# 8 bit codes of x and context: VectorE multiply-add instead of ScalarE Relu in a gated cross-attention and MLP block

## The chip, the cores and the metric

The kernel runs on one core of a Trainium2 chip. The metric is the device time of one execution in microseconds (us). Engines are TensorE (PE; PEld is its weight load), VectorE (DVE), ScalarE (ACT), GpSimd (POOL) and SyncE (SP), which here only issues DMAs.

## What is computed

The reference, cut to what matters (LN is a layer norm without weights):

```python
def fake_quant(x, scale, zp):
    q = jnp.clip(jnp.round(x / scale + zp), 0.0, 255.0)
    return (q - zp) * scale
def attention(x1, x2): return fake_quant(x1, s1, z1) @ fake_quant(x2, s2, z2)

x = x + tanh(g_xattn) * attention(LN(x), ctx)     # x: 2 x 512 x 1024, ctx: 2 x 1024 x 1024
A, g = quant_act(LN(x))                           # fp8 blocks of 16, outliers twice
h = silu(A @ quant_w(w_gate).T * g) * (A @ quant_w(w_up).T * g)      # 2752 columns, int4 blocks of 16
x = x + tanh(g_ffn) * (quant_act(h) @ quant_w(w_down).T * gm)
```

Only the two fake_quant calls, on LN(x) and on ctx, are touched by the change.

## The kernel before

x is 8 tiles of 128 x 1024 (4 for each of 2 batches); ctx is 16 such tiles. Each engine has its own instruction list, written out by hand, and engines meet at semaphores; an instruction whose semaphore is late holds all that stands behind it on its engine.

Front stage (the first 83 us). SP issues the 8 loads of x (`load_x`), the parameters, then `load_ctx(0)` to `load_ctx(6)`. There are 6 context buffers, so `load_ctx(c)` from c = 6 on waits until tile c - 6 has been coded (`ctx_affine`). Behind `load_ctx(6)` SP waits at L376 for `flags_ready`: two flags, made on VectorE from the index inputs, say whether columns are permuted; SP reads both, and takes branches on them. Only then come `load_ctx(7)`, the weight pieces 0, 1 and 2 (`load_piece`, 1 in two halves of 64 partitions) mixed with `load_ctx(8)` and `load_ctx(9)`, then piece 3 and the other contexts.

A context tile goes through three engines: ScalarE turns float32 into uint8 codes (`relu_ctx`, L859, scale and bias in one Relu; the write rounds), GpSimd takes the zero point off and writes bf16 (`shift_ctx`, L702), and TensorE adds it to the column sums (`col_sums`, L1208). The byte buffer `ctx_int` has two slots, hence the wait of tile c for `ctx_quant` c - 1. An x tile goes the same way: `relu_x` on ScalarE (L867) after `layernorm(1)` or `layernorm(2)` on VectorE has made its scale and bias, `quantise_x` on VectorE (L1407, bytes to bf16), `turn_x` on TensorE (L1191), `aT_out` on ScalarE (L873). The statistics of the layer norm are `first_stats(t)` (L1367), two instructions per tile, then `aggregate`.

TensorE's list sets the order: column sums of context tiles 0 to 5, `turn_x(0)`, sums 6 and 7, `turn_x(1)`, sums 8 and 9, `attend(0)` (L1223, 16 matmuls, and L1228), sum 10, `attend(1)`, `turn_x(2)`, sums 11 to 13, `attend(2)`, and so on to `attend(7)`. `make_x1(t)` on VectorE (L1414) adds the result of `attend(t)` to x; `quantise_x(5)` stands behind `make_x1(2)` in VectorE's list, and `turn_x(5)` ahead of `attend(3)` in TensorE's. `col_lo(b)` (L1426) ends the correction term that `attend` adds last.

VectorE's list runs: statistics 0 to 2, parameters, statistics 3 to 5, flag comparisons, `aggregate` of tiles 0 to 3, flag result, `layernorm(1)`, statistics 6 and 7, `aggregate`, `quantise_x(0)`, and then the mix that the diff shows.

Behind the front: second layer norm, fp8 codes of the activations and int4 codes of the first weight pieces on ScalarE, VectorE and GpSimd (83 to 140 us), then TensorE multiplies (L1276, L1330) to the end.

Of the kernel before, what the change touches and what calls it, by code (L numbers as in the profile page):

```python
# [13 lines left out]
ALU = mybir.AluOpType  # L14
ACT = mybir.ActivationFunctionType
# [7 lines left out]
NT = ROWS // P  # L23
# [40 lines left out]
CTX_BUFS = 6  # L64


def gated_block(nc, x, ctx_in, g_xattn, g_ffn, s1, z1, s2, z2, w_gate, w_up, w_down, ri_in, ri_mid, out):
# [4 lines left out]
    with ExitStack() as ctx:  # L72
        def sb(name, shape, dt):
            return ctx.enter_context(nc.sbuf_tensor(name, shape, dt))

        def sem(name):
            return ctx.enter_context(nc.semaphore(name))
# [15 lines left out]
        x_all = big[:, 0:NT * H].rearrange("p (t h) -> p t h", t=NT)  # L93
# [5 lines left out]
        ctx_int = big[:, o:o + H // 2].bitcast(U8).rearrange("p (i n) -> p i n", i=2)  # L99
        x_int = big[:, o + H // 2:o + H].bitcast(U8).rearrange("p (i n) -> p i n", i=2)  # L100
# [23 lines left out]
        ctx_buf = [xn_all[:, 2 + b, :] for b in range(CTX_BUFS)]  # L124
# [23 lines left out]
        prm = sb("prm", [P, 8], F32)  # L148
        pinv = sb("pinv", [P, 2], F32)
# [8 lines left out]
        tt = sb("tt", [P, 8], F32)  # L158
# [5 lines left out]
        ln_mul = sb("ln_mul", [P, NT], F32)  # L164
        ln_add = sb("ln_add", [P, NT], F32)
# [31 lines left out]
        ctx_loaded = [sem(f"ctx_loaded{i}") for i in range(CTX_BUFS)]  # L197
# [6 lines left out]
        ln_ready = sem("ln_ready")  # L204
        x_affine = sem("x_affine")
        a_quant = sem("a_quant")
        a_turned = sem("a_turned")
        aT_ready = sem("aT_ready")
        ctx_affine = sem("ctx_affine")
        ctx_quant = sem("ctx_quant")  # L210
# [629 lines left out]
        def _(act):  # L840
# [7 lines left out]
            def root(n, ts):  # L848
                act.wait_ge(var_ready, n)
                act.activation(sq[:, ts], ve[:, ts], ACT.Sqrt).then_inc(sqrt_done, 1)  # L850

            def relu_ctx(c):

                w = ctx_buf[c % CTX_BUFS]
                act.wait_ge(ctx_loaded[c % CTX_BUFS], 16 * (c // CTX_BUFS) + 16)
                if c >= 2:

                    act.wait_ge(ctx_quant, c - 1)
                act.activation(ctx_int[:, c % 2, :], w, ACT.Relu, bias=prm[:, 3:4], scale=pinv[:, 1:2]).then_inc(ctx_affine, 1)  # L859

            def relu_x(t):

                act.wait_ge(ln_ready, t // 4 + 1)
                if t >= 2:

                    act.wait_ge(a_quant, t - 1)
                act.activation(x_int[:, t % 2, :], x_all[:, t, :], ACT.Relu, bias=ln_add[:, t:t + 1],  # L867
                               scale=ln_mul[:, t:t + 1]).then_inc(x_affine, 1)

            def aT_out(t):  # L870

                act.wait_ge(a_turned, t + 1)
                act.activation(aT[:, :, t * P:(t + 1) * P], tb[t % 2][:].bitcast(BF16).rearrange("p (k r) -> p k r", k=KT),  # L873
                               ACT.Copy).then_inc(aT_ready, 1)

            def col_out(b):

                act.wait_ge(colsum_done, b + 1)
                for hf in range(2):
                    last = act.activation(col_term[0:LO + 1, b, hf * MW:(hf + 1) * MW], col_bank(b, hf)[0:LO + 1, :], ACT.Copy,  # L880
                                          scale=tt[0:LO + 1, 3:4])
                last.then_inc(col_hi, 1)
# [79 lines left out]
                    act.wait_ge(h_done, n - 1)  # L962
                do_silu(n, n, PW if m[0] == "P" else UW)

            relu_ctx(0)
            relu_ctx(1)
            relu_ctx(2)
            root(1, slice(0, 4))
            relu_ctx(3)
            relu_ctx(4)  # L970
            relu_ctx(5)
            relu_x(0)
            relu_ctx(6)
            relu_ctx(7)
            relu_x(1)
            relu_ctx(8)
            relu_ctx(9)
            aT_out(0)
            relu_ctx(10)
            col_out(0)  # L980
            aT_out(1)
            relu_ctx(11)
            relu_x(2)
            relu_ctx(12)
            relu_ctx(13)
            root(2, slice(4, NT))
            relu_ctx(14)
            relu_x(3)
            relu_ctx(15)
            square_x1(0)  # L990
            aT_out(2)
            square_x1(1)
            relu_x(4)
            relu_x(5)
            relu_x(6)
            aT_out(3)
            col_out(1)
            aT_out(4)
            aT_out(5)
            square_x1(2)  # L1000
            relu_x(7)
            round_w(0, 1)
            square_x1(3)
            whole_w(0)
# [350 lines left out]
        def _(dve):  # L1355
            steps = [0]

            def step(ins):

                steps[0] += 1  # L1360
                ins.then_inc(dve_step, 1)
                dve.wait_ge(dve_step, steps[0])
# [7 lines left out]
            def aggregate(ts):  # L1370
                for t in range(ts.start, ts.stop):
                    last = dve.bn_aggr(mv[:, t, :], bst[:, t, :, :])
                step(last)
                dve.tensor_scalar(ve[:, ts], mv[:, ts, 1], EPS, None, ALU.add).then_inc(var_ready, 1)
# [6 lines left out]
            def layernorm(n, ts, mul=2.0, add=None):  # L1381


                r, m = rstd[:, ts], ln_mul[:, ts]
                dve.wait_ge(sqrt_done, n)
                step(dve.tensor_tensor(r, sq[:, ts], sq[:, ts], ALU.mult))
                step(dve.tensor_tensor(r, r, ve[:, ts], ALU.add))
                step(dve.reciprocal(r, r))
                step(dve.scalar_tensor_tensor(out=m, in0=r, scalar=mul, in1=sq[:, ts], op0=ALU.mult, op1=ALU.mult))
                if add is None:  # L1390
                    dve.tensor_tensor(ln_add[:, ts], m, n_mean[:, ts], ALU.mult).then_inc(ln_ready, 1)
                else:
                    step(dve.tensor_tensor(r, m, mv[:, ts, 0], ALU.mult))
                    dve.tensor_scalar(ln_add[:, ts], r, -1.0, add, ALU.mult, ALU.add).then_inc(ln_ready, 1)

            def first_stats(t):

                dve.wait_ge(x_loaded[t], 16)
                return stats(t)

            def quantise_x(t):

                dve.wait_ge(x_affine, t + 1)
                if t >= 2:

                    dve.wait_ge(a_turned, t - 1)
                dve.tensor_scalar(a_nat[t % 2], x_int[:, t % 2, :], nrz[:, 0:1], None, ALU.add).then_inc(a_quant, 1)  # L1407

            def make_x1(t):

                dve.wait_ge(att_done, t + 1)
                for hf in range(2):
                    xs = x_all[:, t, hf * MW:(hf + 1) * MW]
                    last = dve.scalar_tensor_tensor(out=xs, in0=acc[pair(t) + hf][:], scalar=tt[:, 0:1], in1=xs,  # L1414
                                                    op0=ALU.mult, op1=ALU.add, accum_out=x_sum[:, t, hf:hf + 1])
                last.then_inc(x1_ready, 1)
                dve.wait_ge(x1_ready, t + 1)
                dve.tensor_scalar(n_mean[:, t:t + 1], x_sum[:, t, 0:1], x_sum[:, t, 1:2], -1.0 / H, ALU.add, ALU.mult)\
                    .then_inc(mean_ready, 1)
# [168 lines left out]
            dve.tensor_scalar(tt[:, 5:6], pinv[:, 0:1], 2.0, None, ALU.mult)  # L1588
            step(dve.tensor_tensor(tt[:, 1:2], tt[:, 0:1], fz[:, 1:2], ALU.mult))
            dve.tensor_scalar(tt[:, 2:3], tt[:, 1:2], fz[:, 0:1], float(H), ALU.mult, ALU.mult).then_inc(prm_ready, 1)  # L1590
            step(first_stats(3))
            first_stats(4)
            first_stats(5)
            dve.wait_ge(idx_loaded, 32)
            dve.wait_ge(consts_made, 1)
            nm = I // 64
# [3 lines left out]
            dve.tensor_reduce(nfl[:, 0:1], neq[:, 0:8], AX_X, ALU.max).then_inc(flag_step, 1)  # L1600
            dve.tensor_reduce(nfl[0:64, 1:2], neq[0:64, 8:8 + nm], AX_X, ALU.max).then_inc(flag_step, 1)
            aggregate(slice(0, 4))
            dve.wait_ge(flag_step, 5)
            dve.tensor_reduce(nall[:, 0:1], acc[3][:, 0:2 * P], AX_X, ALU.max)
            step(dve.tensor_reduce(nall[:, 1:2], acc[3][:, P:2 * P], AX_X, ALU.max))
            dve.tensor_copy(flag[:], nall[:]).then_inc(flags_ready, 1)
            layernorm(1, slice(0, 4), tt[:, 5:6], prm[:, 1:2])
            first_stats(6)
            step(first_stats(7))
            aggregate(slice(4, NT))  # L1610
            quantise_x(0)
            dve.wait_ge(flags_ready, 1)
            in_moved = dve.value_load(flag[0:1, 0:1], min_val=0, max_val=1)
            quantise_x(1)
            col_lo(0)
            quantise_x(2)
            make_x1(0)
            layernorm(2, slice(4, NT), tt[:, 5:6], prm[:, 1:2])
            make_x1(1)
            quantise_x(3)  # L1620
            quantise_x(4)
            make_x1(2)
            quantise_x(5)
            col_lo(1)
            front_open(0)
            quantise_x(6)
            make_x1(3)
            front_open(1)
            make_x1(4)
# [251 lines left out]
```

## Time and profile before

| | |
|---|---|
| median of 3 runs | 818.23 us (816.87 to 818.39) |
| profiled execution, its own time | 818.77 us |
| its span | 817.0 us, 10350 instructions |
| PE busy | 731.0 us (89%) |
| DVE busy | 556.3 us (68%) |
| ACT busy | 311.3 us (38%), of which L859 19.5 and L867 9.7 |
| POOL busy | 343.7 us (42%), of which L702 18.4 |

Times below are from the span's start. A row of a timeline gives start, duration, engine, line, operation, output and input with their shapes, the number of instructions merged into it, and in brackets how long the engine had been idle and what ended that. A row of the chain gives start, duration, engine and line of a piece of the work that ended last, followed back.

### The profile page before, as it was taken

The numbers are of one execution on the slowest core, as the hardware profiler recorded it, in microseconds if no ns is written. First come the engines' busy times: TensorE is split into PE (matmuls) and PEld (weight loads), VectorE is DVE, ScalarE is ACT, GpSimd is POOL, SyncE is SP. The second block draws the span as 40 slices with busy tenths as digits, with TensorE's granted clock in tenths as the row PEclk, the third lists the DMA queues.
The fourth block names the chain that finished last, engine by engine and source line by source line (L and its number), as shares of the span: only waits on it lengthen the run. The fifth ranks groups of instructions, "written<-read, shape, count | busy, mean of one in ns | idle before, by whom it ended". The sixth has DMA issues, their size and how long they took to land.

```text
span 817.0 us, 10350 instructions
## 1 busy us (share of the span) xinstructions
PE 731.0 (89%) x3473; PEld 334.5 (41%) x3473; DVE 556.3 (68%) x957; ACT 311.3 (38%) x382; POOL 343.7 (42%) x206
## 2 busy tenths in 40 slices
PE   0599003999999999999999999999999999999998
PEld 0144002545444444444444444444444444444443
DVE  5459789894475756675757575745898888988800
ACT  2798972445252524343434343430222122121100
POOL 1536766769374747584848575740000000000000
PEclk9989655999999999999999999999999999999999
DMA  8910598339588897979697969774265654555320
GB/s 308 353 60 14 166 279 147 80 64 190 145 173 212 187 211 174 223 169 227 145 232 163 231 163 236 157 157 164 49 152 162 182 129 149 132 161 121 88 60 26
DMA packets 228884, 131.56 MB, mean 161 GB/s; under 512 B 201712, under 2 KB 212976, under 8 KB 227824
## 3 DMA queue, kind: packets, MB, share of 16 engines
q1 hardware_dynamic: 228848, 131.12, 65.2%
q8 instruction: 18, 0.29, 0.2%
q14 instruction: 18, 0.15, 0.1%
HBM read 61.88 MB, written 19.66 MB: 100 GB/s over the span
## 4 chain that ended last, share of the span: by engine, by line
PE 78%; DVE 5%; POOL 5%; DMA 5%; ACT 3%; SPq 2%; issue 1%; DVEq 0%
PE acc L1276 47%; PE acc L1330 27%; DMA big<-in_ctx_dram 3%; PE acc L1223 2%; POOL big L739 1%; POOL h_in L734 1%; DVE big L1535 1%; ACT wbuf_all L919 1%; POOL wbuf_all L715 1%; POOL wbuf_all L708 1%; POOL big L728 1%; DMA wbuf_all<-in_L_ffn_w_up_dram 1%; SPq L455 1%; DMA mid<-big 1%; DMA x_d<-big 1%
## 5 line engine op out<-in xcount | busy, mean ns | idle before, releaser
L1276 PE MATMUL acc<-mid 128*128 128x512 f16 x1920 | 415.1, 379 | 0.0
L1276 PEld LDWEIGHTS acc<-mid 128*128 128x128 f16 x1920 | 187.9, 98 | 226.1
L1330 PE MATMUL acc<-big,mid 128*128 128x512 f16 x1040 | 224.6, 379 | 0.0
L818 POOL TENSOR_TENSOR h_in<-wbuf_all,h_in 128x1024 f16<-128x1024 f32 (+1 forms) x56 | 114.4, 2044 | 97.2 <-ACT h_in L1115 97.1
L1330 PEld LDWEIGHTS acc<-big,mid 128*128 128x128 f16 x1040 | 101.8, 98 | 122.7
L708 POOL TENSOR_TENSOR wbuf_all<-wbuf_all,w_inv 128x1024 f32<-128x1024 f32 (+1 forms) x67 | 125.2, 1873 | 43.6 <-DVE w_inv L1448 43.6
L1558 DVE SCALAR_TENSOR_TENSOR h_out<-acc,gs,silu 128x256 f32<-128x256 f32 (+1 forms) x88 | 41.5, 471 | 102.6 <-ACT silu L956 65.3
L1442 DVE TENSOR_REDUCE tb<-wbuf_all 128x64 f32<-128x1024 f32 (+1 forms) x67 | 78.9, 1178 | 47.3 <-DMA wbuf_all<-in_L_ffn_w_gate_dram 22.2
L912 ACT ACTIVATE wbuf_all<-wbuf_all 128x1024 f32<-128x1024 f32 (+1 forms) x67 | 68.1, 1016 | 82.2 <-POOL wbuf_all L708 81.4
L1115 ACT ACTIVATE h_in<-wbuf_all 128x1024 f16<-128x1024 f32 (+1 forms) x56 | 56.9, 1016 | 103.1 <-DVE wbuf_all L1454 103.1
L1454 DVE SCALAR_TENSOR_TENSOR wbuf_all<-wbuf_all,tb 128x1024 f32<-128x1024 f32 (+1 forms) x56 | 65.1, 1163 | 0.3 <-issue 0.2
L1153 ACT ACTIVATE wbuf_all<-h_in 128x1408 f16<-128x1408 f32 x16 | 22.0, 1377 | 108.4 <-DVE h_in L1509 67.9
L956 ACT ACTIVATE silu<-acc,gs 128x256 f32<-128x256 f32 (+1 forms) x88 | 40.0, 456 | 50.2 <-PE acc L1276 49.4
L1143 ACT ACTIVATE wbuf_all<-h_in 128x1408 f32<-128x1408 f32 (+1 forms) x16 | 21.6, 1351 | 50.6 <-DVE h_in L1773 50.6
L1276 PE MATMUL acc<-big,mid 128*128 128x384 f16 x192 | 34.4, 341 | 2.1 <-DMA mid<-big 1.3
L1811 DVE SCALAR_TENSOR_TENSOR mid<-acc,hr,mid 128x512 f32<-128x512 f32 x16 | 11.4, 745 | 36.2 <-PE acc L1330 36.2
L1563 DVE TENSOR_REDUCE hm<-h_out 128x256 f32 (+2 forms) x88 | 34.0, 387 | 2.7
L1783 DVE SCALAR_TENSOR_TENSOR h_in<-wbuf_all,h_in 128x1408 f32<-128x1408 f32 (+1 forms) x16 | 25.4, 1587 | 10.1 <-ACT wbuf_all L1143 10.1
L1448 DVE RECIPROCAL w_inv<-tb 128x64 f32<-128x64 f32 (+1 forms) x56 | 30.2, 539 | 1.9
L1223 PE MATMUL acc<-mid,big 128*128 128x512 bf16 x128 | 31.5, 403 | 0.0
L702 POOL TENSOR_SCALAR mid<-big,nrz 128x1024 bf16<-128x1024 uint8 x16 | 18.4, 1151 | 30.4 <-ACT big L859 30.1
L1773 DVE SCALAR_TENSOR_TENSOR h_in<-mid,hr,h_in 128x1408 f32<-128x1408 f32 (+1 forms) x16 | 26.3, 1646 | 0.3
(159 smaller groups left out, 555.0 us busy)
## 6 DMA issues: line engine op xcount, KB each, us to landing
h_in<-h_d SPq DMA_DIRECT2D x8, 1376.0 KB, 7.0
wbuf_all<-in_L_ffn_w_gate_dram SPq DMA_DIRECT2D x21, 512.0 KB, 4.3
wbuf_all<-in_L_ffn_w_up_dram SPq DMA_DIRECT2D x21, 512.0 KB, 4.3
h_d<-h_out SPq DMA_DIRECT2D x80, 128.0 KB, 3.5
big<-in_ctx_dram SPq DMA_DIRECT2D x16, 512.0 KB, 10.7
wbuf_all<-in_L_ffn_w_down_dram SPq DMA_DIRECT2D x16, 512.0 KB, 4.5
big<-in_x_dram SPq DMA_DIRECT2D x8, 512.0 KB, 6.9
x_d<-big SPq DMA_DIRECT2D x8, 512.0 KB, 4.8
```

Source lines behind the costliest of these rows:

```text
L708: pool.tensor_tensor(w, w, spread(w_inv[0:rows, b, 0:cols // BLK]), ALU.mult).then_inc(w_scaled, 1)
L818: last = pool.tensor_tensor(nat[s % 4][:, H:H + cols], wbuf[:, s % 4, 0:cols], nat[s % 4][:, 0:cols], ALU.subtract)
L912: act.activation(wbuf[0:rows, b, 0:cols], wbuf[0:rows, b, 0:cols], ACT.Copy, bias=MAGIC, scale=W_UP)\
L956: act.activation(silu[:, m % 2, 0:cols], acc[m % 4][:, 0:cols], ACT.Silu, scale=gs[:, 2:3]).then_inc(silu_done, 1)
L1115: act.activation(nat[s % 4][:, 0:cols], wbuf[:, s % 4, 0:cols], ACT.Copy).then_inc(nat_hi, 1)
L1223: pe.matmul(acc[pair(t) + hf][:], aT[:, k, t * P:(t + 1) * P], ctxq[:, b * KT + k, hf * MW:(hf + 1) * MW], start=(k == 0), stop=False)
L1276: last = pe.matmul(acc[m % 4][:, 0:cols], left[:, k, s * P:(s + 1) * P], w[:, right, k, 0:cols], start=(k == 0 and left is a_hi and right ...
L1330: last = pe.matmul(acc[2 * i + hf][:], left[:, k - ks.start, :], right[:, k, hf * MW:(hf + 1) * MW], start=(k == 0 and left is hi and righ ...
L1442: dve.tensor_reduce(top, blocks(wbuf[0:rows, b, 0:cols]), AX_X, ALU.max, apply_absolute_value=True).then_inc(scale_step, 1)
L1454: dve.scalar_tensor_tensor(out=w, in0=w, scalar=MAGIC, in1=spread(block_scale(b, looped)[0:rows, 0:cols // BLK]), op0=ALU.subtract, op1=AL ...
L1558: dve.scalar_tensor_tensor(out=h_out[:, m % 2, 0:cols], in0=acc[m % 4][:, cols:2 * cols], scalar=gs[:, 2:3], in1=silu[:, m % 2, 0:cols], o ...
L1563: dve.tensor_reduce(hm[:, s, bass.ds(at, cols // BLK)], blocks(h_out[:, m % 2, 0:cols]), AX_X, ALU.max, apply_absolute_value=True).then_in ...
```

## The change

The 16 `relu_ctx` and 8 `relu_x` leave ScalarE's list. VectorE gets 16 `code_ctx` and 8 `code_x`: a `tensor_scalar` of 128 x 1024, float32 to uint8, multiply by one per-partition scalar and add another. Semaphores are the same; `code_x` needs no wait for `a_quant`, which is VectorE's own. In VectorE's list `first_stats(4)` to `(7)` move behind the flag result and `layernorm(1)`, `code_ctx(0)` to `code_ctx(3)` stand ahead of them, and `quantise_x(0)` to `(4)` and `layernorm(2)` move a little against `make_x1`. Nothing changes on SP, GpSimd and TensorE.

```diff
-            def relu_ctx(c):
-                w = ctx_buf[c % CTX_BUFS]
-                act.wait_ge(ctx_loaded[c % CTX_BUFS], 16 * (c // CTX_BUFS) + 16)
-                if c >= 2:
-                    act.wait_ge(ctx_quant, c - 1)
-                act.activation(ctx_int[:, c % 2, :], w, ACT.Relu, bias=prm[:, 3:4], scale=pinv[:, 1:2]).then_inc(ctx_affine, 1)
...
-            relu_ctx(0)
-            relu_ctx(1)
-            relu_ctx(2)
             root(1, slice(0, 4))
-            relu_ctx(3)
...
+            def code_ctx(c):
+                dve.wait_ge(ctx_loaded[c % CTX_BUFS], 16 * (c // CTX_BUFS) + 16)
+                if c >= 2:
+                    dve.wait_ge(ctx_quant, c - 1)
+                dve.tensor_scalar(ctx_int[:, c % 2, :], ctx_buf[c % CTX_BUFS], pinv[:, 1:2], prm[:, 3:4], ALU.mult, ALU.add)\
+                    .then_inc(ctx_affine, 1)
+
+            def code_x(t):
+                if t % 4 == 0:
+                    dve.wait_ge(ln_ready, t // 4 + 1)
+                dve.tensor_scalar(x_int[:, t % 2, :], x_all[:, t, :], ln_mul[:, t:t + 1], ln_add[:, t:t + 1], ALU.mult, ALU.add)\
+                    .then_inc(x_affine, 1)
...
+            code_ctx(0)
             step(first_stats(3))
-            first_stats(4)
-            first_stats(5)
+            code_ctx(1)
             dve.wait_ge(idx_loaded, 32)
...
             aggregate(slice(0, 4))
+            code_ctx(2)
             dve.wait_ge(flag_step, 5)
             dve.tensor_reduce(nall[:, 0:1], acc[3][:, 0:2 * P], AX_X, ALU.max)
             step(dve.tensor_reduce(nall[:, 1:2], acc[3][:, P:2 * P], AX_X, ALU.max))
             dve.tensor_copy(flag[:], nall[:]).then_inc(flags_ready, 1)
+            code_ctx(3)
             layernorm(1, slice(0, 4), tt[:, 5:6], prm[:, 1:2])
+            code_ctx(4)
+            code_x(0)
+            first_stats(4)
+            code_ctx(5)
+            quantise_x(0)
+            first_stats(5)
+            code_ctx(6)
             first_stats(6)
+            code_ctx(7)
+            code_x(1)
             step(first_stats(7))
+            code_ctx(8)
+            quantise_x(1)
             aggregate(slice(4, NT))
-            quantise_x(0)
+            code_ctx(9)
             dve.wait_ge(flags_ready, 1)
             in_moved = dve.value_load(flag[0:1, 0:1], min_val=0, max_val=1)
-            quantise_x(1)
+            code_x(2)
+            code_ctx(10)
+            quantise_x(2)
             col_lo(0)
-            quantise_x(2)
+            code_ctx(11)
+            code_x(3)
+            layernorm(2, slice(4, NT), tt[:, 5:6], prm[:, 1:2])
+            code_ctx(12)
+            quantise_x(3)
             make_x1(0)
-            layernorm(2, slice(4, NT), tt[:, 5:6], prm[:, 1:2])
+            code_ctx(13)
+            code_x(4)
+            code_ctx(14)
+            quantise_x(4)
+            code_ctx(15)
             make_x1(1)
-            quantise_x(3)
-            quantise_x(4)
+            code_x(5)
+            code_x(6)
             make_x1(2)
             quantise_x(5)
             col_lo(1)
             front_open(0)
             quantise_x(6)
+            code_x(7)
             make_x1(3)
```

## Rows read from the trace of the kernel before

**Rows 1.** Page, part 2: busy tenths in 40 slices of 20.4 us.
```profile
PE   0599003999999999999999999999999999999998
DMA  8910598339588897979697969774265654555320
```

**Rows 2.** Busy time by stretch: stretch, length, us (instructions) per engine, clock, DMA.
```profile
18.70:40.20 21.50, 11.60 (x37) 3.59 (x38) 8.81 (x17) 16.31 (x15) 11.69 (x10) 0.96 1.02 356
40.20:60.20 20.00, 19.43 (x100) 8.29 (x98) 10.72 (x27) 19.31 (x24) 6.71 (x6) 0.88 0.19 75
60.20:83.00 22.80, 22.80 (x170) 10.34 (x168) 21.79 (x45) 19.87 (x26) 14.24 (x7) 1.00 0.07 24
83.00:109.60 26.60, 0.02 (x1) 0.00 (x0) 19.55 (x33) 24.91 (x27) 16.47 (x10) 0.56 0.69 197
```

**Rows 3.** Chain of work that ended last, 12 to 64 us: start, us, what.
```profile
12.58 12.54 DMA big<-in_ctx_dram
26.17 10.50 DMA big<-in_ctx_dram
36.70 1.25 ACT big L859
38.03 1.13 POOL mid L702
...
40.24 5.97 PE acc L1223 x16
...
53.12 3.45 PE acc L1223 x16
...
57.14 1.44 DVE big L1414 x4
...
60.16 3.45 PE acc L1223 x16
```

**Rows 4.** Timeline of SP's DMA issues: context tiles 6 and 7, weight piece 4.
```profile
20.01 0.34 SPq L354 DMA_DIRECT2D big<-in_ctx_dram  x1
...
22.50 0.35 SPq L354 DMA_DIRECT2D big<-in_ctx_dram  x1
...
79.58 0.33 SPq L412 DMA_DIRECT2D wbuf_all<-in_L_ffn_w_gate_dram  x1
```

**Rows 5.** DMA view of the same three issues, in that order: KB, us to landing.
```profile
big<-in_ctx_dram SPq DMA_DIRECT2D x1, 512.0 KB, 6.3
...
big<-in_ctx_dram SPq DMA_DIRECT2D x1, 512.0 KB, 5.0
...
wbuf_all<-in_L_ffn_w_gate_dram SPq DMA_DIRECT2D x1, 512.0 KB, 3.2
```

**Rows 6.** Timeline of DVE.
```profile
12.32 3.81 DVE L1367 BATCH_NORM_STATS2 bst<-big 128x6 f32<-128x512 f32 x6
...
17.43 0.42 DVE L1604 TENSOR_REDUCE nall<-acc 128x1 f32<-128x256 f32 x1 [0.31 <-PE acc L1183]
...
18.09 0.17 DVE L1606 CAST flag<-nall 128x2 int32<-128x2 f32 x1
...
22.86 0.90 DVE L1387 TENSOR_TENSOR rstd<-rstd,ve 128x4 f32<-128x4 f32 x1
...
29.86 0.74 DVE L1407 TENSOR_SCALAR silu<-big,nrz 128x1024 bf16<-128x1024 uint8 x1
...
41.69 1.41 DVE L1426 SCALAR_TENSOR_TENSOR big<-acc,tt,big 1x512 f16<-1x512 f32 x2 [9.56 <-ACT big L880]
...
48.56 0.16 DVE L1387 TENSOR_TENSOR rstd<-rstd,ve 128x4 f32<-128x4 f32 x1
...
111.27 0.49 DVE L1549 TENSOR_SCALAR h_in<-h_in,gs 128x512 f32<-128x512 f32 x1
```

**Rows 7.** Timeline of POOL: two shifts of context tiles.
```profile
22.62 2.35 POOL L702 TENSOR_SCALAR mid<-big,nrz 128x1024 bf16<-128x1024 uint8 x2 [0.23 <-ACT big L859]
```

**Rows 8.** Timeline of ACT: the first three context tiles.
```profile
18.74 3.79 ACT L859 ACTIVATE big<-big,prm,pinv 128x1024 uint8<-128x1024 f32 x3 [6.16 <-DMA big<-in_ctx_dram]
```

More of the change, by code:

```diff
@@ L850, in root @@
                 act.activation(sq[:, ts], ve[:, ts], ACT.Sqrt).then_inc(sqrt_done, 1)
-            def relu_ctx(c):
-                w = ctx_buf[c % CTX_BUFS]
-                act.wait_ge(ctx_loaded[c % CTX_BUFS], 16 * (c // CTX_BUFS) + 16)
-                if c >= 2:
-                    act.wait_ge(ctx_quant, c - 1)
-                act.activation(ctx_int[:, c % 2, :], w, ACT.Relu, bias=prm[:, 3:4], scale=pinv[:, 1:2]).then_inc(ctx_affine, 1)
[L861 to L868, printed above, removed]
             def aT_out(t):
@@ L963, in silu_open @@
                 do_silu(n, n, PW if m[0] == "P" else UW)
-            relu_ctx(0)
-            relu_ctx(1)
-            relu_ctx(2)
             root(1, slice(0, 4))
-            relu_ctx(3)
[L970 to L977, printed above, removed]
             aT_out(0)
-            relu_ctx(10)
             col_out(0)
             aT_out(1)
[L982 to L985, printed above, removed]
             root(2, slice(4, NT))
-            relu_ctx(14)
-            relu_x(3)
-            relu_ctx(15)
             square_x1(0)
@@ L992, in _ @@
             square_x1(1)
-            relu_x(4)
-            relu_x(5)
-            relu_x(6)
             aT_out(3)
@@ L1000, in _ @@
             square_x1(2)
-            relu_x(7)
             round_w(0, 1)
```

## The prediction

> **What bounds the kernel now.** I read the page's slices first. TensorE is full from 140 us to the end, and nothing of the change lies there [rows 1]; the change acts in the first 83 us, so what counts is whether the end of the front stage moves, since what follows hangs on it through data and not through a clock time. Then the busy times by stretch [rows 2]. From 18.7 to 40.2 us the DMA engines are busy all the time (share 1.02) and no engine is full. From 40.2 to 60.2 TensorE is busy 19.4 of 20 us, though ScalarE is too (19.3); from 60.2 to 83.0 TensorE is busy 22.8 of 22.8 us. From 83.0 to 109.6 ScalarE has 24.9 of 26.6 us, with work that the change leaves as it is. Two full engines side by side are told apart by the chain [rows 3]: up to 36.7 us it is loads of context (10.5 us for tile 9), then one code pass of 1.25 us, one shift, and from 40.24 us TensorE's attend steps. ScalarE is full in the middle, but it is not what the others wait for. So its 24 Relus (29.2 us) are worth at most the one of 1.25 us that stands in the chain.
>
> **What a code pass costs on VectorE.** No row shows float32 to uint8 there. The nearest are bytes to bf16, 1024 columns, 0.74 us, and float32 to float32, 512 columns, 0.49 us [rows 6]. The first carries the same number of columns, and the second shows that float32 input runs at a similar rate: with about 0.15 us of it fixed (a 4-column step has 0.16), 1024 columns are 0.15 + 2 x 0.34 = 0.83 us. I take 0.75; bounds are 0.74 and, if bytes out halve the rate, 0.15 + 4 x 0.28 = 1.3 us. 24 passes are 18 us (to 31) on an engine that in 18.7 to 60.2 us had 19.5 of 41.5 us busy. It fits on average; the order decides.
> [...] No row here has float32 to bytes.
>
> **What the order costs: the flags.** Before, VectorE did statistics 3 to 5 from 12.32 us (0.64 each instruction) while it waited for nothing, the flag result ran at 17.43, and the flag cast ended at 18.26 us [rows 6]. Now `code_ctx(0)` stands ahead of statistics 3 and waits for the first context tile, which lands at 18.7 us [rows 8]. Then: code 0 to 19.5; statistics 3 to 20.75; code 1 to 21.5; comparisons and reduces, small steps of 0.15 to 0.2, and aggregate, to 22.4 or, held by a shift (below), 23.0 to 23.7; code 2 to 23.7 or 24.45; flag reduces 0.6, cast 0.17. `flags_ready` comes at 25.1 to 25.9 in place of 18.26, at best 24.3 if nothing is held.
> SP has issued context tile 6 and stands at that wait, with tile 7, the weight pieces, and every later load queued behind it. Before, the flags had long been there, and reading them and branching took from 20.35 to 22.50 us, that is 2.15 us [rows 4]. Now tile 7 is issued at 25.1 to 25.9 + 2.15 = 27.3 to 28.0 us. Tile 6, issued at 19.6, lands at 26.3 as before, so the DMA queue is empty by then; a load into an empty queue takes 3.2 us [rows 5]. Tile 7 lands at 30.5 to 31.2 in place of 27.5: +3.0 to +3.7. Tile 9 landed 36.67 - 27.5 = 9.2 us behind tile 7, with DMA busy throughout [rows 2, 3]; kept, it lands at 39.7 to 40.4.
>
> **GpSimd and VectorE hold each other.** L1387 took 0.90 us at 22.86 and 0.16 at 48.56; the first ended at 23.76, when the first of the two shifts begun at 22.62 (1.15 us each or so) ended [rows 6, 7]. The same op alone is short, so a VectorE op of such a kind waits out a shift, up to 1.1 us. Every code pass starts a shift on GpSimd, so what comes two places behind it can be held; one directly behind starts first, since an instruction follows on its own engine without a gap, and a shift 0.1 us after its semaphore.
> [...]
>
> **The sum on VectorE.** With cast at 25.1: code 3 to 25.8; layernorm(1), one step held, to 28.0; code 4, code_x(0) to 29.45; statistics 4 to 30.7; code 5, quantise(0) to 32.15; statistics 5 to 33.4; code 6 to 34.15; statistics 6 to 35.35; code 7, code_x(1) to 36.85; statistics 7 to 38.1; code 8, quantise(1) to 39.55; aggregate, its last step held, to 40.9; code 9 to 41.6 (tile 9 is there by 40). With the cast at 25.9 it is 42.4. Shift 9 (1.13), two column sums and attend(0) follow: 44.0 to 44.7 us in place of 40.24 [rows 3], +3.7 to +4.5. Loads and VectorE end within 2 us of each other there, so either alone would cost 2.5 us and more.
> Then TensorE: attend(0) 6.0 + 0.5 at the low clock as before, sum 10, attend(1), turn, sums, attend(2) to 61.0 to 61.8 us, where it was 57.12. Beside it VectorE does code_x(2) (held once), codes 10 to 15, col_lo(0) 1.4, layernorm(2) (held), code_x(3) to (6), quantise(2) to (4) and make_x1(0), (1) at about 1.6 each: back to back from 41.6 it reaches make_x1(2) at 61 to 62.5. So it is late by 0 to 1 us against attend(2); I take 0.6. make_x1(2), quantise(5), turn and attend(3) take 3.04 us (57.12 to 60.16) as before. code_x(7) 0.75 falls where VectorE waited 0.84 us for ScalarE in `col_lo(1)`, which now need not: nothing. attend(3) to (7) run back to back on TensorE, and what follows moves with them.
> What is gained: 1.25 to 0.75 us in the chain once, already in the sum. ScalarE's freed 29 us lie beside other work. Total +3.7 to +4.5, mean 4.1, and 0.6: +4.7 us. On the profiled execution that is 818.8 + 4.7 = 823.5; it was 0.5 above the median, so 822.9 against 818.23.
>
> **Rivals.**
> [...] 0.13.
> (b) The pass runs at half the rate, 1.3 us. 23 passes up to quantise(5) add 12 us, less some holding: +13, 831 us. Against it stands bytes in at 0.74. 0.05.
> (c) No change: the slow stretch from tile 7 to 9 (2.5 MiB in 9.2 us) runs at the rate of the loads ahead of it (1.3 us for 0.5 MiB, 6.4 us), which wins 2.8 us back, and VectorE is not held. About 819, 0.12.
> [...] 0.08.
> That the codes are not what the Relu gave (rounding, negatives) would change values and no time.
>
> **How the numbers follow.** Forecast 822.9, with its own range 820.5 to 825, chance 0.62. The range to hold the time 8 times in 10 goes to most of (a) and to the lower edge of the forecast and part of (c): 819.5 to 828; left out are (d), (b) and half of (c). A measurement of this kernel tells 0.2% (1.6 us) from nothing. Slower: forecast, (a), (b), 0.80; same: (c), 0.12; faster: (d), 0.08.
>
> **What would show it.** The flag cast at 24 to 26 us; SP's issue of tile 7 at 27 to 28; a dip of the DMA share between 26 and 30; code passes of 0.75 us, some small VectorE steps near 1 us; attend(0) at 44 to 45, attend(3) at 64 to 66, last attend matmul at 87 to 88 in place of 83; ScalarE idle most of 20 to 60 us and no gain from it; the stretch from there to the end as long as before. The prediction is wrong if the passes are not 0.75 us, if tile 9 lands by 38 us, or if what follows attend(7) shrinks by microseconds.

## The result, and the profile after

The change makes the kernel slower: 824.03 us (median of 5 runs, 822.26 to 826.49) against 817.69 us, ratio 1.0077 with a 95% interval of 1.0053 to 1.0100, that is +6.3 us. The forecast was 822.9 us (+4.7 on the 818.23 of the first measurement), range 819.5 to 828. A second measurement of the same kernel, below, gives 1.0072. The profiled execution is the lowest of the five: 822.26 us, span 820.5, where the profiled execution of the kernel before is 1.1 us above its median (818.77 against 817.69). So the two traces lie 3.5 us apart where the medians lie 6.3.

The changed kernel's busy times by stretch, cut where [rows 2] has its stages, each moved by what the stage moved (stretch, length, us (instructions) per engine PE, PEld, DVE, ACT, POOL, clock, DMA share, GB/s):

```profile
18.00:42.60 24.60, 11.85 (x39) 3.78 (x40) 23.06 (x49) 3.60 (x6) 13.07 (x10) 0.71 0.87 308
42.60:62.70 20.10, 18.44 (x100) 8.03 (x99) 19.69 (x38) 6.36 (x9) 9.01 (x6) 0.93 0.23 90
62.70:88.00 25.30, 24.69 (x173) 10.88 (x170) 24.71 (x47) 19.12 (x25) 15.01 (x8) 0.93 0.06 21
88.00:113.60 25.60, 0.08 (x1) 0.00 (x0) 18.71 (x31) 24.06 (x27) 15.67 (x9) 0.54 0.71 204
```

ScalarE fell from 16.3 and 19.3 us [rows 2] to 3.6 and 6.4, and VectorE rose from 8.8 and 10.7 to 23.1 and 19.7 us: it is now the full engine from the first context tile to attend(3). The DMA share of the first stretch fell from 1.02 to 0.87. The dip lies where the late flags hold the loads: from 24 to 28 us the share is 0.26, before it was 0.98.

The first part of the chain (start, us, what), which answers to [rows 3]:

```profile
9.44 8.49 DMA big<-in_ctx_dram
17.96 0.81 DVE big L1365
...
23.33 0.68 DVE flag L1581
24.03 0.47 SPq L377
...
31.32 10.90 DMA big<-in_ctx_dram
...
42.97 0.75 DVE silu L1381
43.75 1.40 DVE big L1400 x2
...
66.30 2.34 DVE big L1372
```

Up to 42 us it runs through the flag cast (L1581), SP's reading of the flags (L377), and a load (that of context tile 10, issued at 31.32); from there on through VectorE, where before TensorE's attend steps stood. VectorE's timeline shows the pieces, with context codes at L1365, x codes at L1372 and bytes to bf16 at L1381:

```profile
17.96 0.81 DVE L1365 TENSOR_SCALAR big<-big,pinv,prm 128x1024 uint8<-128x1024 f32 x1 [6.38 <-DMA big<-in_ctx_dram]
...
23.33 0.67 DVE L1581 CAST flag<-nall 128x2 int32<-128x2 f32 x1
...
39.67 0.81 DVE L1365 TENSOR_SCALAR big<-big,pinv,prm 128x1024 uint8<-128x1024 f32 x1 [1.02 <-DMA big<-in_ctx_dram]
40.62 1.62 DVE L1372 TENSOR_SCALAR big<-big,ln_mul,ln_add 128x1024 uint8<-128x1024 f32 x1
...
66.22 2.42 DVE L1372 TENSOR_SCALAR big<-big,ln_mul,ln_add 128x1024 uint8<-128x1024 f32 x1
```

A pass that is not held takes 0.81 us; one directly behind another starts 0.72 us after it (26.30 and 27.02 us). The row at 39.67 is context tile 9: VectorE waited 1.02 us for it. Context tile 7 and tile 9 on SP's timeline:

```profile
26.11 0.35 SPq L354 DMA_DIRECT2D big<-in_ctx_dram  x1
...
29.94 0.41 SPq L354 DMA_DIRECT2D big<-in_ctx_dram  x1
```

Tile 7 is issued 3.6 us later than before [rows 4] and takes 3.6 us to land in place of 5.0; tile 9 lands at 29.94 + 9.7 = 39.6 us, 3.0 later. And TensorE's attend(0) and attend(3):

```profile
42.59 5.06 PE L1181 MATMUL acc<-mid,big 128*128 128x512 bf16 x16
...
62.70 3.62 PE L1181 MATMUL acc<-mid,big 128*128 128x512 bf16 x16
```

On that timeline they stood at 40.03 and 60.00 us before. So the traces are 2.6 us apart at attend(0), 2.7 at attend(3), 4.0 at the first multiply of the MLP (143.66 against 139.68) and 3.5 at the end. The time from the first multiply to the end of the span is 676.8 us, before 677.3: in these two executions all of the difference is made in front.

### The profile page after: what moved, and what is told of

Its sections match the earlier page's. It is cut to its first block, busy times and chain, and to the rows that moved or that the text cites. A ratio compares the mean times of both kernels' runs of the same rounds, so it can differ in the third digit from the quotient of the medians.

```text
span 820.5 us, 10344 instructions
## 1 busy us (share of the span) xinstructions
PE 731.2 (89%) x3473; PEld 334.6 (41%) x3473; DVE 576.4 (70%) x981; ACT 284.0 (35%) x358; POOL 347.5 (42%) x206
## 4 chain that ended last, share of the span: by engine, by line
PE 77%; DVE 9%; DMA 3%; POOL 3%; ACT 3%; issue 2%; SPq 2%; DVEq 0%
PE acc L1234 49%; PE acc L1288 27%; DMA big<-in_ctx_dram 2%; POOL big L728 1%; DVE big L1509 1%; DVE big L1388 1%; POOL big L739 1%; POOL h_in L734 1%; DVE big L1365 1%; DMA wbuf_all<-in_L_ffn_w_up_dram 1%; DMA x_d<-big 1%; DVE big L1372 1%; SPq L347 1%; ACT wbuf_all L901 0%; DVE tb L1416 0%
## 5 line engine op out<-in xcount | busy, mean ns | idle before, releaser
L702 POOL TENSOR_SCALAR mid<-big,nrz 128x1024 bf16<-128x1024 uint8 x16 | 22.1, 1380 | 32.8 <-DVE big L1365 32.8
```

## The experiments

Ratios are to the kernel before, with a 95% interval; kernels that are compared ran against a common pool of runs of it. "attend(0)" and the like are the starts of its matmuls on TensorE's timeline in each kernel's one profile. The first context tile lands anywhere from 17.2 to 19.0 us in these traces, whatever the kernel, so single starts are good to about 1 us.

| kernel | median us | ratio | attend(0) | attend(3) | first multiply |
|---|---|---|---|---|---|
| before | 817.1 to 818.0 | 1 | 40.0 | 60.0 | 139.7 |
| changed | 824.03 | 1.0077 (1.0053 to 1.0100) | 42.6 | 62.7 | 143.7 |
| after_again | 823.25 | 1.0072 (1.0059 to 1.0085) | 42.9 | 63.1 | 143.9 |
| flags_first | 821.61 | 1.0046 (1.0033 to 1.0058) | 40.4 | 60.4 | 142.7 |
| x7_early | 821.95 | 1.0057 (1.0038 to 1.0076) | 42.7 | 62.8 | 143.0 |
| flags_and_x7 | 819.86 | 1.0028 (1.0017 to 1.0039) | 41.2 | 60.6 | 140.7 |
| flags_late_before | 822.42 | 1.0056 (1.0039 to 1.0073) | 44.2 | 64.1 | 143.7 |
| ctx_only | 822.73 | 1.0055 (1.0037 to 1.0073) | 43.2 | 62.8 | 143.4 |
| x_only | 817.14 | 0.9989 (0.9978 to 1.0001) | 38.8 | 57.9 | 138.5 |
| shift_on_act | 824.72 | 1.0076 (1.0054 to 1.0097) | 43.1 | 64.3 | 146.8 |
| ctxfirst_after | 821.56 | 1.0054 (1.0040 to 1.0069) | 42.4 | 62.0 | 142.5 |
| ctxfirst_before | 812.89 | 0.9944 (0.9930 to 0.9957) | 34.7 | 54.0 | 133.9 |
| ctxfirst_x_only | 812.56 | 0.9941 (0.9928 to 0.9954) | 36.0 | 53.4 | 133.6 |

**The changed kernel again.**

> The changed kernel once more, to see how far its trace differs from one execution to the next (its five times went from 822.3 to 826.5 us, and the profiled one was the lowest, 3.5 us above the one of before, where the medians are 6.3 us apart). If the part that varies lies in the front stage, this profile shows attend(0), attend(3) or the first multiply at another time than 42.6, 62.7 and 143.7 us, because a VectorE op met a GpSimd op where it did not before, or the other way round. If it is spread of the chip, the front stage has the same times within 0.3 us and the difference lies behind 143 us. Ratio to before 1.005 to 1.010 in both cases.

The front stage is the same to 0.4 us (attend(0) 42.93, first multiply 143.87, span 820.9), and this profile too is from the fastest of its runs (822.65 of 822.65 to 825.08). So neither theory is decided: the slower executions, up to 826.5 us, are not seen in a trace. Their mean granted clock does not sort them (822.26 us at 0.952, 826.49 at 0.961).

**The flags put back ahead of code_ctx(0).**

> The changed kernel with one part undone: statistics 3, the comparisons and the flag result stand ahead of code_ctx(0) again, so flags_ready comes before the first context tile lands. Theory (the late flags cost about half of the loss, because they hold context tile 7 and all loads behind it): tile 7 is issued at 22 to 22.7 us, tile 9 lands at 36.7, VectorE reaches code 9 at 37 to 38 because the flag work now lies in its idle time, attend(0) starts at 40 to 40.6 in place of 42.6, and 2 to 2.6 us go: 821.5 us on a scale where the changed kernel is 824.0 and before 817.7, ratio 1.0045. Rival 1 (VectorE's own 18 us of passes are the limit and the loads are not): attend(0) stays within 0.7 us of 42.6, 823.5 to 824. Rival 2 (the flags are the whole loss): 818, ratio 1.000.

```diff
-            code_ctx(0)
             step(first_stats(3))
-            code_ctx(1)
...
             aggregate(slice(0, 4))
-            code_ctx(2)
             dve.wait_ge(flag_step, 5)
...
+            code_ctx(0)
+            code_ctx(1)
+            code_ctx(2)
             code_ctx(3)
```

1.0046, attend(0) at 40.4 us: as the theory had it. Tile 7 is issued at 21.57 us again, and VectorE no longer waits for tile 9 but comes to it late (its timeline; the row is code 9):

```profile
21.57 0.35 SPq L354 DMA_DIRECT2D big<-in_ctx_dram  x1
```
```profile
37.01 0.80 DVE L1365 TENSOR_SCALAR big<-big,pinv,prm 128x1024 uint8<-128x1024 f32 x1
```

Tile 9, issued at 24.18, had landed at 35.2 (11.0 us); VectorE reached it 1.8 us later, with no idle time ahead of it. Part of the early start is the early first context tile (17.16 us here). In the kernel with both edits, below, whose list up to here is the same, that tile landed at 18.0 and attend(0) came at 41.2. So the late flags are worth 1.4 to 2.2 us of the 2.6 at attend(0).

At attend(3) this kernel is only 0.4 us behind the one before, with all 24 passes on VectorE. What it still loses comes behind that: code_x(7) takes 2.42 us here too, and the first multiply is 3.0 us late.

**The flags delayed in the kernel before.**

> The kernel before with one added wait on VectorE: statistics 3 and all behind it wait for the first context tile, as they do in the changed kernel; all code passes stay on ScalarE. flags_ready comes at 24 to 25 in place of 18.3 us. Theory (the flags alone delay the loads and through them everything): tile 7 is issued at 26 to 27.3 us, tile 9 lands 2.5 to 3.3 us later than before, attend(0) and the end move by the same, 820.2 to 821, ratio 1.003 to 1.004. Rival (the loads behind the flags have slack, and it is the passes on VectorE that cost): within 0.3 us of before, ratio 1.000.

```diff
+            dve.wait_ge(ctx_loaded[0], 16)
             step(first_stats(3))
```

1.0056: the late flags by themselves cost the kernel before +4.5 us (interval 3.2 to 6.0), more than the theory's 2.5 to 3.3. Tile 7 is issued 4.0 us late, and the delay goes through undiminished: attend(0) is 4.2 us late (TensorE waits 5.09 us for the shift of tile 9), the first multiply 4.0.

```profile
26.50 0.35 SPq L354 DMA_DIRECT2D big<-in_ctx_dram  x1
```
```profile
44.20 5.91 PE L1223 MATMUL acc<-mid,big 128*128 128x512 bf16 x15
```

Tile 9 landed at 30.18 + 10.7 = 40.9 us. In the changed kernel, with flags about as late, it landed 1.2 us earlier and attend(0) began 1.6 us earlier, of which 0.4 is the shorter code pass (0.81 for 1.25 us).

**code_x(7) moved ahead of front_open(0).**

> The changed kernel with code_x(7) moved ahead of front_open(0) (it now waits for a_quant 6, which is its own engine's). In the changed kernel it stood right behind front_open(0), whose last step starts a GpSimd scale of 2.3 us, and took 2.42 us. Theory (it was held by that scale, and make_x1(3), (4) and all that follows came late by it): it takes 0.8 us, make_x1(3) starts at 67 in place of 68.6 us, make_x1(4) follows attend(4) at once, and 1.2 to 1.6 us go: 822.5, ratio 1.0058. Rival (something later absorbs or replaces it, such as quantise(6) being held in its place): 824.0, ratio 1.0077.

```diff
             col_lo(1)
+            dve.wait_ge(a_quant, 6)
+            code_x(7)
             front_open(0)
             quantise_x(6)
-            code_x(7)
             make_x1(3)
```

The pass and make_x1(4) on VectorE (L1388), in this kernel:

```profile
63.73 0.81 DVE L1372 TENSOR_SCALAR big<-big,ln_mul,ln_add 128x1024 uint8<-128x1024 f32 x1
...
71.06 0.75 DVE L1388 SCALAR_TENSOR_TENSOR big<-acc,tt,big 128x512 f32<-128x512 f32 x1 [0.40 <-PE acc L1186]
```

0.81 us in place of 2.42, and make_x1(4) waits for TensorE again. The median is 2 us lower and the ratio 1.0057 as expected, though its interval overlaps that of the changed kernel; so this run alone does not show the gain. In the traces 1.4 us of it is there at the root behind make_x1(4) (75.23 against 76.62 us): quantise(7) took 2.46 us in place of 1.15, but the step behind it (L1337) 0.16 in place of 1.89. At the first multiply 0.7 is left; in between VectorE waits for the up weights (until 106.38 us here, 107.05 in the changed kernel).

**Both together.**

> The changed kernel with both undone: the flag result ahead of code_ctx(0), and code_x(7) ahead of front_open(0). Alone the first gave back 2.3 us of about 6 (1.0046 for 1.0072 to 1.0077) and the second 1.5 (1.0057). Theory (two separate costs, one ahead of attend(0), one behind attend(3)): the gains add, 1.003, that is 820 us, and make_x1(4) starts at 68.7 to 69.2 us, within 0.9 us of before. Rival (both act on the same later limit, ScalarE's list from root(3) on): no better than the better of the two alone, 1.0045.

The edits are the two above.

1.0028 (1.0017 to 1.0039), against 1.0046 and 1.0057 for either alone: the gains add, and the rival's 1.0045 lies outside the interval. Against flags_first this kernel prices code_x(7) better than x7_early does: attend(3) stands within 0.2 us of it, the root 1.8 us earlier (73.28 for 75.11) and the first multiply 2.0. Of the loss of 6 us, some 2.3 are left. The trace has 1.0 of it at the first multiply and 0.5 at the end of the span; where the rest lies is not shown.

**The shifts moved to ScalarE.**

> The changed kernel with the 16 shifts of context (bytes to bf16) moved from GpSimd to the now idle ScalarE, 1.25 us each in place of 1.12. No GpSimd op runs between 3 and 65 us, so nothing there can hold VectorE. Theory (holding costs VectorE some 5 us spread over 20 to 60 us, of which only what comes after the last slack counts): no VectorE pass over 0.85 us before 60 us, the flag cast 0.17 in place of 0.67, flags 0.5 to 0.7 us earlier, attend(0) at 42 to 42.5, attend(3) at 61.5 to 62.2 in place of 62.7, 822.6 to 823.4, ratio 1.006 to 1.007. Rival 1 (holding is the main cost of VectorE's list): attend(3) at 60 us, 821. Rival 2 (it is not holding that makes those passes long): they stay at 1.5 to 1.6 us.

```diff
-            shift_ctx(0)
...
-            shift_ctx(15)
             scale(0, 1)
...
+            def shift_act(c):
+
+                act.wait_ge(ctx_affine, c + 1)
+                act.activation(ctxq[:, c, :], ctx_int[:, c % 2, :], ACT.Identity, bias=nrz[:, 1:2]).then_inc(ctx_quant, 1)
...
+            shift_act(0)
             root(1, slice(0, 4))
+            shift_act(1)
...
```

(and so on to `shift_act(15)` in ScalarE's list.) Up to 60 us everything that was long on VectorE's timeline is short; the flag cast and code 9:

```profile
23.34 0.17 DVE L1586 CAST flag<-nall 128x2 int32<-128x2 f32 x1
...
40.21 0.81 DVE L1370 TENSOR_SCALAR big<-big,pinv,prm 128x1024 uint8<-128x1024 f32 x1 [2.96 <-DMA big<-in_ctx_dram]
```

Rival 2 falls: GpSimd's shifts did hold VectorE. But the time is 1.0076 (1.0054 to 1.0097), no better, and the median of 824.72 us misses the expected 822.6 to 823.4. VectorE now waits 2.96 us for tile 9, which landed at 40.2 us although its issue, at 29.29, was 0.65 earlier (10.9 us in flight for 9.7). Behind that my own order costs: the last three shifts stand behind aT_out(2) in ScalarE's list, and attend(2) waits for one of them (57.3 us in place of 54.7). So this run tells what the holding is, and nothing of its price.

**Each half of the change.**

> The other half: the 16 context passes on VectorE in the changed order (flags late), the 8 passes over x on ScalarE. Theory (late flags, then a list with 6 us less on it and nothing for the scale to hold behind front_open(0)): tile 7 issued at 26 to 27, attend(0) at 42.3 to 43, attend(3) at 62.2 to 63, and 1.5 us less than the changed kernel behind that: 822.2, ratio 1.0055. Rival (VectorE's total work is the limit): attend(3) at 60 to 61, 820, ratio 1.003.

```diff
 # from the changed kernel: all code_x leave VectorE's list, relu_x is back on ScalarE
+            relu_x(0)
+            relu_x(1)
             aT_out(0)
...
-            code_x(0)
             first_stats(4)
...
```

1.0055, as expected: the context half carries the late flags and loses 4.5 us, as much as the delayed flags alone do. VectorE waits 3.11 us for tile 9 here, so the loads set attend(0), not its list. The 1.5 us that were expected behind attend(3) do not show in the traces: the first multiply is 0.3 us earlier than in the changed kernel.

> Half of the change: only the 8 passes over x go to VectorE (each waits for its own engine's quantise two tiles back), context and the whole order up to the flags as in the kernel before. Theory (ScalarE's full list was beside the loads and TensorE): tile 7 issued at 22.5, tile 9 lands at 36.7, attend(0) at 40.2, attend(3) at 60.2, and the time is that of before within 0.7 us, ratio 0.999 to 1.001. Rival 1 (ScalarE was a limit, and 10 us less on it show): 816 or less, ratio 0.998. Rival 2 (passes on VectorE hold GpSimd's shifts and are held): 819 or more, ratio 1.0015 and up.

```diff
 # from the kernel before: all relu_x leave ScalarE's list
-            relu_x(0)
...
             layernorm(1, slice(0, 4), tt[:, 5:6], prm[:, 1:2])
+            code_x(0)
             first_stats(6)
+            code_x(1)
             step(first_stats(7))
...
```

0.9989 (0.9978 to 1.0001): no loss, and at most a gain of 0.2%, which the interval does not set apart from none. TensorE was busy 19.43 of 20 us between 40.2 and 60.2 us, as before, with ScalarE at 15.0 in place of 19.3:

```profile
40.20:60.20 20.00, 19.43 (x107) 8.59 (x106) 15.81 (x33) 15.04 (x20) 6.23 (x6) 0.95 0.18 70
```

The ratio is at the edge of the expected 0.999 to 1.001, the positions are not as expected: attend(0) came at 38.8 us in place of 40.2, attend(3) at 57.9 in place of 60.2. Neither comes from ScalarE's shorter list. Tile 9 landed 0.9 us earlier (26.01 + 9.8 = 35.8 us), ScalarE coded it at once (35.84), as before, and the column sums and attend(0) ran faster (0.63 and 5.30 us for 1.03 and 6.17). At the end of the span nothing of it is left (817.0 us in both).

**All contexts loaded ahead of the flags and the weights.**

> The kernel before with SP's order changed: load_ctx(7) to load_ctx(15) stand directly behind load_ctx(6), ahead of the wait for the flags and of all weight pieces. Nothing else. Theory (loads, not ScalarE's full list, set the start of attend(0)): tile 9 lands at 30 to 31 us, ScalarE's 12 passes from 18.7 us end at 32.5 and are now the limit, attend(0) starts at 34.5 to 35.5 in place of 40.2, and all behind moves with it: 812.5, ratio 0.9935. Rival (ScalarE, busy 19.3 of 20 us in the middle, is a limit right behind the loads): attend(0) gains 5 us and attend(3) 2 or less, 815.5 to 816, ratio 0.997.

```diff
             load_ctx(6)
+            load_ctx(7)
...
+            load_ctx(15)
             sp.wait_ge(flags_ready, 1)
```

(with the same nine calls taken out from among the weight pieces). 0.9944, 812.89 us: faster than both kernels. The theory holds: the loads set attend(0). Its rival's numbers fall: attend(3) moves by 6.0 us with attend(0) by 5.3.

```profile
34.74 3.62 PE L1223 MATMUL acc<-mid,big 128*128 128x512 bf16 x16
```

attend(0) even took 3.62 us in place of 6.17, with TensorE granted 1.00 over that stretch (0.58 before, from 40.0 to 46.2 us). So attend(0) ended 7.8 us earlier, and only 6.0 of that reach attend(2) and attend(3). The chain shows what took the rest:

```profile
43.70 1.13 ACT big L859
44.84 1.13 ACT hm L890 x2
45.97 0.92 ACT big L873
46.93 3.63 PE acc L1223 x16
```

TensorE waits 1.66 us ahead of attend(2) for `aT_out(2)` (L873), which stands behind the last code pass in ScalarE's list. As soon as the loads are out of the way, ScalarE's full list is a limit, as the rival had it, though for 1.7 us and not for 3 and more.

> The same order of loads with the x half of the change: context coded on ScalarE, x on VectorE. Theory (work split between the two engines lets each keep up with the loads): context tiles are coded as they land, tile 9 at 31.5 us, attend(0) at 33.5 to 34.5, 811 to 812, ratio 0.992, some 1 us better than with all passes on ScalarE. Rival (VectorE's passes are held by the shifts, which now come more densely): no better than 812.5 or worse.

The edit is that of ctxfirst_before on top of x_only.

0.9941, no different from 0.9944: the theory's 811 to 812 us are missed, and the number is the rival's. attend(0) began at 36.0 us, later than with all passes on ScalarE: the chain there runs through code_x(0), code_x(1) (held, 1.43 us), statistics, aggregate and quantise(0) on VectorE to turn_x(0) at 31.85 us (29.96 with all passes on ScalarE). The shorter list of ScalarE wins this back: TensorE no longer waits ahead of attend(2), and attend(3) stands at 53.4 us against 54.0.

> The same order of loads with all 24 passes on VectorE, in the changed order and with code_x(7) ahead of front_open(0), as in x7_early (ratio 1.0057). The flags are as late as in the changed kernel but hold only the weight pieces. Theory (VectorE's own list is a second limit just under the late flags): every context tile is there when VectorE comes to it, code 9 starts at 38.5 to 39 in place of 39.7, attend(0) at 41 to 42, and only about 1 us goes: 821 to 821.8, ratio 1.0045. Rival (the late flags and loads were all of the front's loss): attend(0) at 35 to 37 us, 815 to 817, ratio 0.998 or less.

The edit is that of ctxfirst_before on top of x7_early.

1.0054, attend(0) at 42.4 us: the theory holds. Here code 9 follows without a wait:

```profile
39.03 0.80 DVE L1365 TENSOR_SCALAR big<-big,pinv,prm 128x1024 uint8<-128x1024 f32 x1
39.76 0.80 DVE L1372 TENSOR_SCALAR big<-big,ln_mul,ln_add 128x1024 uint8<-128x1024 f32 x1
40.48 1.61 DVE L1365 TENSOR_SCALAR big<-big,pinv,prm 128x1024 uint8<-128x1024 f32 x1
```

With the loads out of the way VectorE's list alone sets attend(0), at 42.4 us where ScalarE's list reached 34.7. In that order of loads the passes on VectorE cost 8.7 us (821.56 less 812.89). The statistics and the flag work still stand behind code_ctx(0) in this list, so the 8.7 us are those of the passes in the changed order; the same loads with the flag work ahead of code_ctx(0) were not run.

## Why the prediction was right

**What bounds the kernel.** Right. x_only took a third of the passes off ScalarE and moved nothing that can be told from noise; ctxfirst_before left all of them there and gained 4.6 us by loads alone. In the kernel before, ScalarE's 19.3 of 20 us were beside the path. That holds only as long as the loads come late: in ctxfirst_before the same list costs TensorE 1.7 us.

**The pass.** Right. Taken as 0.75 us; it is 0.81 us, 0.72 from start to start. Rival (b), half the rate, falls.

**The flags.** Right in mechanism, and 1 us too late. The cast was put at 25.1 to 25.9 and ended at 24.0; tile 7 was put at 27.3 to 28.0 and went out at 26.1; reading the flags and branching took 2.1 us (24.0 to 26.1), as taken. The difference: 0.8 us because the first context tile landed at 17.96 in place of 18.74, and the shift that was to hold the comparisons and the aggregate for 0.6 to 1.3 us held one step of them, L1332, for 0.23 (0.40 us for 0.17). Against that the cast was held for 0.5. Tile 9 landed 3.0 us late, the lower end of +3.0 to +3.7. flags_late_before confirms the term by itself.

**Two limits side by side.** Half right: "either alone would cost 2.5 us and more". The flags alone cost 4.5 us in the kernel before; taken out of the changed kernel they give back only 2.3; and with the loads out of the way VectorE's list still holds attend(0) at 42.4, 2.4 us behind the kernel before. But in flags_first and flags_and_x7, where only the list was left, attend(3) is 0.4 and 0.6 us late, since the statistics and the flag work run there while VectorE would wait for the first context tile. So both limits have one source: work that the kernel before did ahead of that tile was put behind it.

**attend(0) and attend(3).** Put at 44.0 to 44.7 and 64 to 66, they came at 42.6 and 62.7. Besides the 1.1 us of the flags, attend(0) was shorter (5.06 us for 6.17 on the timelines), where the prediction took it "at the low clock as before". No run shows a clock that stays from kernel to kernel: TensorE was granted 0.71 over attend(0), 0.58 before and 1.00 in ctxfirst_before (3.62 us). Nor does the granted clock tell the length in every trace: flags_first has 1.00 over its 6.2 us. So attend(2) was only 1.7 us late (54.68 against 52.95), for 3.9 to 4.7 in the prediction. make_x1(2) then began at 59.85, 1.0 us behind the end of attend(2), because VectorE's list came to it late; I had taken 0.6. Together that is the +2.7 us at attend(3).

**The holding.** That a shift holds a VectorE op was read from one row, L1387, and the runs show it: the same step, in layernorm(2), took 0.89 us at 46.83 in the changed kernel (L1345), where it ended with the shift of 46.10 (1.61 us), and 0.16 in shift_on_act, without shifts on GpSimd. So does the cast at 23.33 (0.67 us, 0.17 in shift_on_act). It is not so for every op: the two statistics at 18.69 us, beside the shift of 18.87, took 1.28 us, as they did in shift_on_act. Right, too, is that the pass directly behind a code pass starts ahead of the shift: code_ctx(4) began at 26.30 us and ended at 27.11, code_x(0) began at 27.02 and the shift at 27.20. Rival (a), in which such a pass waits for the shift, falls, and no run shows the 1.1 us apiece that it took into the upper end of the range: no pass directly behind a code pass was held, and GpSimd's shift took longer instead (1.55 to 1.62 us for 1.12 at nine of the sixteen). Held were passes two places behind, at 53.10 and 55.30 us, and the one behind a gap, at 40.62.

**The term that was mis-sized.** "code_x(7) 0.75 falls where VectorE waited 0.84 us for ScalarE in col_lo(1): nothing." It does not cost nothing. I looked for holding by the shifts only, which end at 58 us, and not by what GpSimd does next. front_open(0) ends with the scale factors that start `scale(0, 1)`, and the pass stands two places behind it, the very case that the prediction describes:

```profile
65.81 2.28 POOL L708 TENSOR_TENSOR wbuf_all<-wbuf_all,w_inv 128x1024 f32<-128x1024 f32 x1 [7.69 <-DVE w_inv L1422]
```

The scale ends at 68.09, the pass at 68.64: 2.42 us for 0.81. That put make_x1(3) and (4) late and turned +2.7 us at attend(3) into +4.1 at the root behind make_x1(4) (76.62 against 72.47). With code_x(7) moved the root comes 1.4 us (x7_early) or 1.8 us (flags_and_x7 against flags_first) earlier. So the errors had opposite signs: 2.0 us too much up to attend(3) (+4.7 for +2.7), 1.4 too little at code_x(7).

**Behind attend(3).** "attend(3) to (7) run back to back on TensorE, and what follows moves with them" is not the path of the changed kernel. From make_x1(3) to the root the chain stays on VectorE. TensorE waited 0.61 us and ran attend(7) in 5.30 us for 3.61, so that it ended 5.0 us late (88.1 for 83.0), and this cost nothing: VectorE came to make_x1(7) at 90.38 us, 2.3 behind the end of attend(7).

**The rest.** +4.0 us at the first multiply is what the traces show; the medians say +6.3. Both profiles of the changed kernel fell on its fastest run. Where the slower ones lose their 2 us is not shown. Nor is it shown that the change makes the time spread more: its five runs cover 4.2 us, but so do 23 runs of the kernel before (816.21 to 820.42). So the closeness of 822.9 to 824.03 is in part luck: two misses of 2.0 and 1.4 us with opposite signs in the traced stages, and 1.8 us between the traced run and the median that nothing explains. The traced run lies 1.2 us below the 823.5 that the prediction gave for it, the median 1.1 above its 822.9.

**The other rivals.** (c) and (d) fall. The slow stretch of loads won only 0.8 us back, not 2.8: tile 9 was issued 3.8 us late and landed 3.0 late. In (d) attend(0) runs shorter and the kernel gains by it. attend(0) did run 1.1 us shorter in the changed kernel, which is 6.3 us slower all the same; in flags_first, where tile 7 went out at 21.57 us, attend(0) took 6.2 us (40.40 to 46.59), as before, and the kernel stayed slower than before.

## What to carry to other kernels

A full engine beside a full DMA queue or TensorE is not a reason to move its work: read from the chain what ends last, and test with a run that takes the suspected limit away (here, nine loads moved ahead of a wait gained 4.6 us and left the full engine full, 18.5 of 19.3 us). Then look again, since the full engine may be the next limit: here it held TensorE for 1.7 us as soon as the loads no longer did. When passes are put into another engine's list, follow what they push back, above all small results that some other queue waits for: with all 24 passes on VectorE but the flag result back in its place, attend(3) was 0.4 to 0.6 us late in place of 2.7. Ahead of attend(3) it is less the 18 us of passes that cost than a flag of two elements that came nearly 6 us later and held every load behind it. And on VectorE look at what GpSimd is released to do just ahead of each inserted pass (here a scale of 2.28 us, beside which a pass of 0.81 took 2.42), not only at the partner that the change itself creates.

## What the runs showed of the hardware that was not expected

A GpSimd op is stretched by VectorE as well, which the prediction's sum did not price: the shift of 1.12 us took 1.55 to 1.62 in the nine places of the changed kernel where a second code or byte pass stood right behind the code pass that released it. The two engines then took turns: where a third such pass followed at once, the waiting shift went first and that pass was held (code_ctx(14), 1.62 us at 53.10, behind code_x(4) at 52.38, with the shift from 52.56 to 54.18).

A load of 512 KB in the same place of the queue (context tile 9, issued between 24.2 and 31.0 us) took 8.7 to 11.0 us to land from one kernel's trace to the next; in the two traces of the changed kernel it took 9.7 and 9.9. The first context tile landed between 17.2 and 19.0 us. So one profile places a load-bound event to about 1 us only.
